# Self attention on one core: the next entry's norm three periods earlier, its projections, rotation and splits at other steps, and the largest score tiles first

## The reference, cut to what matters

```python
for l in range(N_LAYERS):                      # 4
    h = rmsnorm(x, n1[l])
    qkv = h @ Wqkv[l].T + bqkv[l]
    q, k, v = jnp.split(qkv, 3, axis=-1)
    q = apply_rope(split_heads(q, H), cos, sin)    # H = 16 heads of 8
    k = apply_rope(split_heads(k, H), cos, sin)
    v = split_heads(v, H)
    o = merge_heads(sdpa(q, k, v, causal_bias)) @ Wo[l].T + bo[l]
    x = x + o
    ...                                        # cross attention, gated FFN
```

## Time and profile before

| what | us |
|---|---|
| median of 3 runs | 2355.92 |
| lowest, highest | 2351.07, 2369.44 |
| the profiled execution | 2364.77 |
| its span, first to last instruction | 2363.0 |
| four self attentions, from the first to the last maximum of each | 205.5, 197.0, 197.1, 197.2 |

### The profile page before, as it was taken

How to read it: one execution, slowest core, us unless ns; L and a number is a source line. 1 busy time by engine, 2 the same in 40 slices (tenths; PEclk the granted TensorE clock), 3 DMA queues, 4 the chain that set the end, 5 groups by cost and what they waited for, 6 DMA issues and landing times.

```text
span 2363.0 us, 34847 instructions
## 1 busy us (share of the span) xinstructions
PE 2048.8 (87%) x13610; PEld 1236.0 (52%) x13610; DVE 1510.8 (64%) x3724; ACT 1063.8 (45%) x1412; POOL 540.5 (23%) x761
## 2 busy tenths in 40 slices
PE   6977999699876598899988999998999998889977
PEld 4556665466553344455544455554456554456553
DVE  7546655444776666774576775467776467777468
ACT  2543555222253155555245645345545435555510
POOL 1111000000122344320234420144430034421020
PEclk9988999799987588999989989989989989989988
DMA  4001000000000000000000000000000000000000
GB/s 160 13 1 54 1 12 1 14 1 1 1 1 12 1 1 1 1 10 1 25 1 1 2 1 10 12 14 1 1 1 10 1 14 1 1 1 10 1 1 18
DMA packets 13331, 24.46 MB, mean 10 GB/s; under 512 B 4072, under 2 KB 9584, under 8 KB 12528
## 3 DMA queue, kind: packets, MB, share of 16 engines
q1 hardware_dynamic: 13168, 22.24, 2.9%
HBM read 21.19 MB, written 1.05 MB: 9 GB/s over the span
## 4 chain that ended last, share of the span: by engine, by line
PE 46%; DVE 11%; issue 5%; ACT 3%; POOL 1%; DVEq 0%; POOLq 0%
PE wide L611 33%; PE acc L611 13%; DVE maxima L1488 3%; ACT prob L1702 2%; DVE hn L1084 1%; POOL rstd L1755 1%; DVE hid L1015 1%; DVE x L1549 1%; ACT prob L1631 1%; ACT q_g L1574 0%; DVE moments L1050 0%; DVE maxima L1172 0%; DVE A L1015 0%; DVE hn L1086 0%; DVE qkv L1447 0%
## 5 line engine op out<-in xcount | busy, mean ns | idle before, releaser
L1488 DVE TENSOR_REDUCE maxima<-wide 128x2 f32<-128x512 f32 (+3 forms) x512 | 405.0, 819 | 172.3 <-PE wide L611 167.4
L1702 ACT ACTIVATE prob<-wide 128x768 f32<-128x768 f32 (+1 forms) x384 | 334.1, 882 | 213.5 <-PE wide L611 212.9
L1631 ACT ACTIVATE prob<-wide 77x1024 f32<-77x1024 f32 x256 | 260.4, 1019 | 145.2 <-PE wide L611 145.0
L611 PE MATMUL wide<-q_g 32*128 32x256 f32 (+3 forms) x2048 | 270.8, 414 | 52.9 <-DVE maxima L1488 19.6
L1172 DVE TENSOR_REDUCE maxima<-wide 128x8 f32<-128x616 f32 x256 | 203.0, 795 | 168.4 <-PE wide L611 166.7
L1875 POOL TENSOR_SCALAR_AFFINE_SELECT prob<-prob 128x256 f32<-128x256 f32 (+1 forms) x384 | 183.6, 483 | 379.7 <-ACT prob L1702 379.5
L1755 POOL TENSOR_TENSOR rstd<-moments,cst 128x4 f32<-128x4 f32 x88 | 89.6, 1018 | 764.5 <-issue 351.0
L611 PEld LDWEIGHTS wide<-q_g 32*128 32x128 f32 x2048 | 142.0, 197 | 228.7 <-issue 109.9
L611 PE MATMUL wide<-q_g,kx 128*77 128x512 f32 x512 | 254.8, 570 | 5.0 <-DVE hid L1404 2.0
L1574 ACT ACTIVATE q_g<-wide 128x1024 fp32r<-128x1024 f32 x128 | 131.2, 1025 | 219.6 <-PE wide L611 219.6
L611 PE MATMUL wide<-kx,q_g 128*128 128x312 f32 x512 | 179.5, 415 | 10.4 <-DVE maxima L1172 9.9
(11 more groups left out here) (217 smaller groups left out, 3279.3 us busy)
## 6 DMA issues: line engine op xcount, KB each, us to landing
A<-in_w SPq DMA_DIRECT2D x2, 2048.0 KB, 12.7
unit_w<-in_unit_w SPq DMA_DIRECT2D x8, 448.0 KB, 3.3
ffn_w<-in_ffn_w SPq DMA_DIRECT2D x4, 768.0 KB, 5.5
unit_w<-in_unit_rows SPq DMA_DIRECT2D x8, 192.0 KB, 3.8
x<-in_x SPq DMA_DIRECT2D x4, 256.0 KB, 4.8
att_w<-in_att_w SPq DMA_DIRECT2D x4, 256.0 KB, 2.6
att_w<-in_att_rows SPq DMA_DIRECT2D x4, 256.0 KB, 3.3
A<-in_gate SPq DMA_DIRECT2D x1, 1024.0 KB, 4.9
```

The lines of the kernel that those rows point to most:

```text
L611: return e.matmul(out, lhsT, rhs, start=start, stop=stop, is_transpose=turn)
L1488: e.tensor_reduce(top[:, t, h], v[:, :, at0:at0 + P * t + P], AX.X, ALU.max, negate=True).then_inc(*made("max", *([("free", tile)] if t == ...
L1631: e.activation(p[0:SC, :], s[0:SC, :], ACT.Exp, bias=0.0, scale=1.0).then_inc(*made("exp", pb, ("free", tile)))
L1702: e.activation(pv, sv, ACT.Exp, bias=0.0, scale=8 ** -0.5).then_inc(*made("exp", pb, ("free", tile)))
```

## The change

`CAUSAL_TILES` is reversed in size. For entry b+1 the norm moves three periods up, to the period (b-1, 2) (for entry 1 to the period (0, 0)), at rows 4 and 12. Its turn and projections stay in the period (b, 1), at rows 0, 4 and 10. The rotation has four operations in the period (b, 2), rows 0, 4, 8, 12, and two in (b, 3), rows 2 and 6. `cut_q` moves to row 12 of the period (b, 3), `cut_k` to row 4 of (b+1, 0). Nothing is added to or taken from any engine's work.

```diff
--- before.py
+++ after.py
@@ -222,7 +222,7 @@
 
 
 
-CAUSAL_TILES = [((0, 1), (1,)), ((2, 3), (1,)), ((0, 1), (2, 0)), ((2, 3), (2, 0)), ((0, 1), (3,)), ((2, 3), (3,))]
+CAUSAL_TILES = [((0, 1), (3,)), ((2, 3), (3,)), ((0, 1), (2, 0)), ((2, 3), (2, 0)), ((0, 1), (1,)), ((2, 3), (1,))]
 
 
 
@@ -237,21 +237,27 @@
 
 
 def self_steps(l):
+    def normalise(b):
+        return in_rows((4, ("stats", "s", l, b)), (12, ("apply", "s", l, b)))
+
     def project_in(b):
-        return in_rows((0, ("stats", "s", l, b)), (2, ("apply", "s", l, b)), (6, ("turn", "s", l, b)),
-                       (10, ("qkv", l, b, 0)), (12, ("qkv", l, b, 1)))
-
-    def rotate(b, part):
-        return in_rows(*[(row, ("rotate", l, b, 3 * part + k)) for k, row in enumerate((2, 6, 10))])
+        return in_rows((0, ("turn", "s", l, b)), (4, ("qkv", l, b, 0)), (10, ("qkv", l, b, 1)))
 
     def prepare(b, g):
         if (b, g) == (0, 0):
-            return in_rows((0, ("cut_q", l, b)), (2, ("cut_k", l, b)), (8, ("qk_turn", l, b, g)))
+            return beside(in_rows((0, ("cut_q", l, b)), (2, ("cut_k", l, b)), (8, ("qk_turn", l, b, g))), normalise(1))
         rows = in_rows((8, ("qk_turn", l, b, g)))
         if g == 0:
-            return beside(rows, in_rows((0, ("cut_q", l, b)), (2, ("cut_k", l, b))))
-        if b + 1 < B:
-            rows = beside(rows, project_in(b + 1) if g == 1 else rotate(b + 1, g - 2))
+            rows = beside(rows, in_rows((4, ("cut_k", l, b))))
+        elif b + 1 < B:
+            if g == 1:
+                rows = beside(rows, project_in(b + 1))
+            elif g == 2:
+                rows = beside(rows, in_rows(*[(4 * k, ("rotate", l, b + 1, k)) for k in range(4)]))
+                rows = beside(rows, normalise(b + 2)) if b + 2 < B else rows
+            else:
+                rows = beside(rows, in_rows((2, ("rotate", l, b + 1, 4)), (6, ("rotate", l, b + 1, 5)),
+                                            (12, ("cut_q", l, b + 1))))
         return rows
 
 
@@ -280,7 +286,9 @@
 
     items = [[prepare(b, g), scores(b, g), attend(b, g), finish(b, g)] + ([project_out(b)] if g == G - 1 and b + 1 < B else [])
              for b in range(B) for g in range(G)]
-    return project_in(0), [in_rows(*[(row, ("rotate", l, 0, row)) for row in range(6)])], items
+    begin = in_rows((0, ("stats", "s", l, 0)), (2, ("apply", "s", l, 0)), (4, ("turn", "s", l, 0)), (6, ("qkv", l, 0, 0)),
+                    (8, ("qkv", l, 0, 1)))
+    return begin, [in_rows(*[(row, ("rotate", l, 0, row)) for row in range(6)])], items
 
 
 def program_order():
```

## The result

The changed kernel takes 2391.55 us (median of 4 runs, 2387.78 to 2392.17) against 2359.16 for the kernel before beside it: ratio 1.0132, interval [1.0088, 1.0175]. A repeat in another session gave 1.0095 [1.0075, 1.0115]. It is slower by about 1%. The forecast was 2305, range 2280 to 2338.

A forecast was written before the change was run, and what follows sets the result against it. PE was taken as the bound, with only its waits and half clock recoverable. Won 43.4 (waits) + 26.5 (clock) + 2.4 (clean intervals), lost 21.2: net 51 us, 2314 against the profiled execution, 2305 against the median; range 2280 to 2338.

The forecast's parts named there:

- the clock's part: Stretches, intervals (1,0) to (3,0) of each layer: half-clock time costs at most 31.2 us, of which 26.5 was counted won.
- the new waits of the stretches: Per stretch 5.3 us lost: three splits 3.75, norm of entry 3 0.8, rotation 2 x 0.4; 21.2 us in four layers.
- Part 5: Layer entry, (0,1) to (0,3): about 1 us new wait at entry 1's turn against waits and low clock there; put at 0.
- Part 4: Largest tiles first: `self_full`'s 0.17 us wait goes in (3,1) to (3,3), 2.4 us won; k = 0, 1 hold slots 0.54 longer.
- the walks above: Following DVE's queue against PE's need in (b,2) and (b+1,0): new waits of 0.5 us at the stats, 1.25 at the splits.
- Parts 1 and 3: Norm three periods up with earlier turn and projections (1), and POOL's rotation with four operations in (b,2) (3): their new waits.
- Norm of entry 3 0.8: New waits per stretch from that norm: 0.5 us at the stats in (b,2), 0.3 to 0.5 at the apply before `o_norm`.
- Rotation 0.4 per entry: Fourth POOL rotation, at row 12 of (b,2), meets DVE's fill: 0.4 us lost per entry, bounds 0 and 1.3.
- the floor: About 0.4 us per interval that PE misses even in clean intervals such as (3,2) and (1,3); not counted as winnable.
- the signs of being wrong: PE waiting at row 4 for k = 0, clock below 0.95 in the stretches, or a layer entry above 34 us.
- (a): Rival: DVE becomes the bound in the stretches, waits only move and half the clock's part is lost; 2331 us, chance 0.16.
- (c): Rival: slower, block 3's tiles first make PE stop at row 4's logits tile for k = 0; 2377 us, chance 0.05.

The follow-up runs named there:

- both_rows: apply_g3 with the rotation at rows 2, 6, 10 of (b,2) and 2, 5, 8 of (b,3), stats at row 8: 2321.56 us, ratio 0.9815.
- turn_late: Changed kernel, norm of entry 1 still early, its turn and projections back at rows 6, 10, 12 of period (0,1): 2360.08 us, ratio 0.9965.
- entry_tiles_old: Changed kernel with the old tile order and entry 1's norm, turn and projections at their old rows in period (0,1): 2349.36 us, ratio 0.9963.
- apply_g3: entry_tiles_old with the norm's apply moved from row 12 of period (b,2) to row 4 of (b,3): 2339.48 us, ratio 0.9895.
- rot_rows2: apply_g3 with the rotation at rows 2, 6, 10 of (b,2) and 2, 5, 8 of (b,3): ratio 0.9837.
- moves_only: Changed kernel with the old tile order: 2364.54 us, ratio 0.9987.

## Why the prediction was wrong

The forecast was right on most waits of the stretches and on the splits. It failed on the steps quoted below. The profiled execution came out 78 us above its 2314. Of these, 36 are the clock's part in the stretches, 18.4 the entries, 8.7 the intervals (3,1) to (3,3), 4.6 the new waits of the stretches, and 10.5 stand outside them all, which the forecast had put at nothing. The first two carry the sign.

**"Of the clock's part I count 85%, 26.5 us."** Nothing came: half-level time in the stretches was 62 us before and 67 and 64 after, and PE was busy 9.6 us longer (410.7 for 401.1) instead of 26.5 shorter. I had tied this return to the waits that go (2.14 and 1.23 us) and priced the new waits by their length alone. But there are new waits of 1.07 us, four a layer, and of the 19 waits between 0.9 and 1.3 us 16 had a fall beside them. That a return of 0 was possible stood there as a bound; it should have been a rival with a high chance, as the sum of the waits and the clock's part hang on different things. When 48 of the 62 us at half level were really gone (both_rows) PE was busy 385.0 us in the stretches for 401.1 before: 16 us. For all 62 that makes about 21, an estimate, so the 26.5 was too high as well.

**Part 5, "I put 0, bounds 3 lost and 5 won per layer."** Measured 4.6 us lost per layer (18.4 / 4), outside the bounds, 3.6 of it idle: PE waits 2.2 us at the turn and 2.3 at the fill, where before it waited 1.1 for ACT's copy and 0.4 at the fill. I had named the first wait and called it 1 us. The second I missed: I followed the projection to its new row and not what it had covered at the old one, nor that an earlier projection lets POOL's rotation start beside the fill (1.51 us for 0.37). turn_late shows that these steps make the difference between slower and faster.

**Part 4, "nothing where DVE is on time; where it is late, this is in the walks above."** Of the gain of 2.4 us a third came: (3,2) takes 9.46 us for 9.66, while (3,3) stayed at 10.69, and so did (3,1) at full clock (10.05). The price was not nothing: 0.5% alone, 0.7% on entry_tiles_old, 1% on all moves. The walks had the 0.3 us, at no price of their own.

**Parts 1 and 3, sizes.** "Norm of entry 3 0.8" measured about 1.6 in the kernel after: (1,2) idles 1.99 us and (2,2), without a norm, 0.91; (1,3) 0.86 and (2,3) 0.38. With the old tile order it is 2.1: the apply in front of `o_norm`, which I priced at 0.3 to 0.5, costs 1.4 there (apply_g3). "Rotation 0.4 per entry" was near in the kernel after, where (2,2) idles 0.91 us, 0.5 over the floor, and (2,3) 0.38. With the old tile order it is 0.96: rot_rows2 takes 0.56 us of idle from (2,2) and 0.40 from (2,3). I saw the meeting at row 12 and missed the one at row 0. The rule of the Trainium skill (SBUF — State Buffer, Who interferes with whom) weighed in part 3 would have added up to 10 us to my price. The trace agrees with it: the fill begun at 1236.53 beside POOL's operation ends at 1237.28, with it (1236.19 + 1.05 = 1237.24). In the kernel after, all new waits of a stretch together idle 6.4 us over the floor for my 5.3; with the old tile order my 1.6 us a layer for norm and rotation was too low by 2.4 (2.06 + 2 x 0.96 for 1.6).

**Right:** the waits of (1,1) and (2,1) (2.9 and 2.8 to 0.8 and 0.6); the splits, with a wait of 1.07 where I had 1.25; the stretches' waits as a whole, 17.6 us won for 43.4 - 21.2 = 22.2 forecast. The places are those that the forecast named; in the total, sizes offset in part (the splits took 3.3 us a stretch for 3.75, the norm 1.6 for 0.8). And (1,1) and (2,1), forecast near 12.2 us at full clock, take 13.22 and 14.19 on average.

Of the signs of being wrong two came: the clock of the stretches was 0.94, 0.90, 0.96 and 0.90, which was to be (a), and three of the four entries took over 34 us (44.88, 36.21, 33.55, 36.22; layer 0's took 38.83 before). Of the rivals none was it. (a) is nearest: waits that lower the clock again. But it kept half of the clock's part and left the entry at 0. (c) named the right direction and a part of the cause, the tiles of block 3 in front (0.5% alone), but by another wait: in the stretches PE waits at most 0.44 us at any tile for a maximum other than the transposes, not 0.9.

**Open:** why a wait of about 1 us is followed by a fall in one kernel and less often in another; how the tile order costs 17 us when the stretches idle the same; and the clock outside the edited stages, which moved the single traces by 15 us.

## What to carry to other kernels

When PE is the bound and the low clock stands beside its waits, look at how long each wait is and not only at their sum: an edit that turns few waits of 2 us into more of 1 us may win nothing. For each step that moves, ask what it covered at its old row and what will stand behind it on its engine at the new one: here a projection over a fill, and an apply in front of `o_norm`. And try a bundle of moves one by one; these moves, with the stats, the apply and the rotation placed otherwise and with the tile order and the early steps of entry 1 left out, are worth 1.8%, and as a bundle they cost 1%.

## What the runs showed of the hardware that was not expected

- In these self attentions the granted clock fell during, or within 2.5 us after, every one of 97 waits of PE of 1.8 us or more that began at full clock, and 65 of 112 between 0.9 and 1.3 us. Of an execution, 328 (both_rows) to 451 us (after) were at 1.2 GHz.
- Executions of one kernel can lie 24 us apart, and the granted clock goes with it: moves_only ran from 2347.45 us (clock 0.928) to 2371.15 (0.916), in ten runs. The difference in clock is some 57 us at half level, which at 0.34 to 0.48 us each (next point) makes 19 to 27 us, an estimate.
- What a us at the half level cost was not one number. In the stretches PE's busy time was 401.1 us before with 62 at half level and 410.7 after with 67, for 385.0 with 14 in both_rows: 0.34 and 0.48 us per further us at half level. PE waited more in the kernel before (57.6 for 40.0 us); that this is the reason isn't shown.
- DVE's small fill operations, 0.18 and 0.19 us alone, took 0.75 (entry_tiles_old) and 0.98 (after) beside POOL operations and ended with them, while the norm's stats kept their 0.87 us beside a rotation (after, 1256.83, beside POOL's 1.05 us from 1256.88).
